# Two transformer layers with mixture-of-experts on one core: the shared expert moved into the last stage, and gathers held to two in flight

## The chip, the cores and the metric

The kernel runs on 1 core of one Trainium2 chip. The metric is the device time of one execution in microseconds (us). Before the change it is 1326.83 us, the median of 3 runs (1325.98 to 1328.25).

The core has five engines with instruction queues of their own: TensorE (PE in the profile, with its weight loads as PEld), VectorE (DVE), ScalarE (ACT), GpSimd (POOL) and SyncE (SP, used only to issue DMAs). They wait for each other through semaphores: a finished instruction adds 1, a landed DMA adds 16. A queue is in order, so whatever stands behind a waiting instruction waits too.

## The reference, cut to what matters

The input is x with 4 x 512 tokens of 256 values. The program computes, in order:

```python
x0 = layernorm(x)           # layer 0: attention with 16 heads, and a mixture of 32 experts, 4 per token
x  = x + attn0(x0) + moe0(x0)
x1 = layernorm(x)           # layer 1: attention (4 heads) and a mixture of experts on the same normalised input
xf = rmsnorm(x1) * norm_w
routed = sum over the token's 4 experts of weight * (silu(xf @ w1[e]) * (xf @ w3[e])) @ w2[e]
shared = (silu(xf @ shared_gate_w) * (xf @ shared_up_w)) @ shared_down_w
out = x + x1 + attn1(x1) + routed + shared
```

Each expert has 256 slots in layer 1; a token that finds its expert full is dropped there. The change is about `shared` and about how `routed` is collected at the end. `routed` needs, for each token, the four rows that its experts wrote, times the token's four weights.

## The kernel before, in words

A program is a row of blocks, and all engines meet in a barrier between two of them. In order: `norm_block0`, `route_block` (layer 0), `attention_block0` for batches 0 and 1, `expert_block` (layer 0), `attention_block0` for batches 2 and 3, `norm_block1`, `route_block` (layer 1), `attention_block1`, `expert_block` (layer 1), `combine_block1`. The order inside a block is written out by hand for each engine, and it is the order of the loops in the code. There is no planner.

Tokens lie in 16 tiles of 128; a batch has four of them. `s.x` is the residual in SBUF, `s.xn` the normalised input of the experts, with tokens on the partitions. `xfT` is the same with columns on the partitions, as TensorE wants it; it is made by 32 transpositions of 128 x 128.

**norm_block1** (its body is printed below). SP issues 15 loads: the raw query weights, a bias, norm weight and gate (`w_in`), the three weights of the shared expert (`w_in` too, lines 1349 to 1351), and then the attention's other weights (`attn_in`). VectorE normalises (L1393) and makes `s.xn` (L1401). TensorE transposes both (L1441), ScalarE copies them out (L1416), TensorE computes the logits (L1426). POOL waits for all ten `attn_in` loads, adds up the query weights of four groups (L1368 to L1370, and three small ones for the bias) and then adds the normalised input to the residual (L1377, four instructions).

**route_block, layer 1**. VectorE finds each token's four experts, counts and ranks with TensorE's help, and has the slots ready at L744. Only then can POOL scatter the rows of `s.xn` into `xs` in HBM: 64 indirect DMAs (L761), of which 24 stand in this block and 40 in `attention_block1`. In the same block TensorE projects queries, keys and values of each batch (`project`, L599 and L604), VectorE takes them out (`take`), ScalarE makes their high parts (L513, L515), POOL their low parts (L471, L472), and SP stores all six parts of a batch in HBM. POOL's order is: low parts of batch 0; then for each further batch eight scatters and the two low parts.

The shared expert stands in this block as well, batch by batch: `gate_up` on TensorE (L613), Silu on ScalarE (L523), the product `hidden` on VectorE (L664), `down` on TensorE (L623) and the add to the residual `add_down` on VectorE (L670).

**attention_block1** and **expert_block** compute attention and the routed experts; the latter writes one row per slot into `ys` in HBM.

**combine_block1** is the last stage. POOL issues 64 indirect DMAs (L1700), tile by tile and choice by choice, each of which gathers 128 rows of 256 values from `ys` into a place of its own in `big_a`. VectorE waits for the four gathers of a tile and adds them to the residual with their weights (L1712). SP stores the output two tiles at a time (L1693). TensorE and ScalarE have nothing to do there.

Of the kernel before, what the change touches and what calls it, by code (L numbers as in the profile page):

```python
# [20 lines left out]
ALU = mybir.AluOpType  # L21
# [300 lines left out]

def shared_weights(s):

    w = s.probs[:].rearrange("p a n -> p (a n)")
    at = 0
    views = []
    for width in (EMB, KC * EXPERTS, KC * I1, KC * I1, EMB):
        views.append(w[:, at:at + width])
        at += width  # L330
    nw, gate, sg, su, sd = views
    gate, sg, su = (a.rearrange("p (k n) -> p k n", k=KC) for a in (gate, sg, su))
    return nw, gate, sg, su, sd
# [10 lines left out]
def route_block(nc, s, d, layer, xs_zeroed=None):  # L344
# [51 lines left out]
    else:  # L396
        _, _, sg, su, sd = shared_weights(s)
        xfT = s.big_b[:, 0:KC * TOKENS].rearrange("p (k n) -> p k n", k=KC)
        silu, hid = s.probsT[:, 0:2 * SEQ].rearrange("p (a n) -> p a n", a=2), s.khb
# [3 lines left out]
        UP_BANK, V_BANK, Q_BANK, KA_BANK, KB_BANK, GATE_BANK = s.ps[2:8]  # L403
        DOWN_BANKS = (RANK, small)
        q_full, k_full = s.big_a[:, 0:SEQ], s.big_a[:, SEQ:2 * SEQ]

    with signals(nc, f"r{layer}") as sem, ExitStack() as ctx:
# [7 lines left out]
        projected, taken, gated, silu_done, hid_ready, down_done, x_added = map(  # L415
            sem, ("projected", "taken", "gated", "silu", "hid", "down", "x_added"))
# [67 lines left out]
        def _(act):  # L484
# [22 lines left out]
            else:  # L507
# [10 lines left out]
                split_high(0)  # L518
                for c in range(BATCH):
                    act.wait_ge(gated, c + 1)  # L520
                    if c >= 2:
                        act.wait_ge(hid_ready, c - 1)
                    a(silu[:, c % 2], GATE_BANK[:, :], ACT.Silu).then_inc(silu_done, 1)  # L523
                    if c + 1 < BATCH:
                        split_high(c + 1)

        @block.tensor
        def _(pe):
# [79 lines left out]
            def gate_up(c):  # L608
                if c:
                    pe.wait_ge(hid_ready, c)  # L610
                for bank, wt in ((GATE_BANK, sg), (UP_BANK, su)):
                    for k in range(KC):
                        mm = nc.tensor.matmul(bank[:, :], wt[:, k, :], xfT[:, k, c * SEQ:(c + 1) * SEQ],  # L613
                                              start=k == 0, stop=k == KC - 1)
                mm.then_inc(gated, 1)

            def down(c):
                pe.wait_ge(hid_ready, c + 1)
                for half, bank in enumerate(DOWN_BANKS):
                    if c:  # L620
                        pe.wait_ge(x_added, 2 * (c - 1) + half + 1)
                    for i in range(2):
                        mm = nc.tensor.matmul(bank[:, i * EMB:(i + 1) * EMB],  # L623
                                              hid[:, c % 2, (2 * half + i) * P:(2 * half + i + 1) * P], sd,
                                              start=True, stop=True)
                    mm.then_inc(down_done, 1)

# [3 lines left out]
            gate_up(0)  # L631
            tile_row()
            for b in range(1, BATCH):
                project(b)
                if b == 1:
                    pe.wait_ge(row_read, 1)
                down(b - 1)
                gate_up(b)
            down(BATCH - 1)

        @block.vector
        def _(dve):
# [16 lines left out]

            def hidden(c):  # L660
                dve.wait_ge(silu_done, c + 1)
                if c >= 2:
                    dve.wait_ge(down_done, 2 * (c - 1))
                v.tensor_tensor(hid[:, c % 2], silu[:, c % 2], UP_BANK[:, :], ALU.mult).then_inc(hid_ready, 1)  # L664

            def add_down(c):
                for half, bank in enumerate(DOWN_BANKS):
                    dve.wait_ge(down_done, 2 * c + half + 1)
                    t = 4 * c + 2 * half
                    v.tensor_tensor(s.x[:, t:t + 2, :], s.x[:, t:t + 2, :],  # L670
                                    bank[:, :].rearrange("p (t e) -> p t e", t=2), ALU.add).then_inc(x_added, 1)
# [645 lines left out]
def norm_block1(nc, s, d):  # L1317
# [4 lines left out]
    nw, gate, sg, su, sd = shared_weights(s)  # L1322
# [4 lines left out]
    with signals(nc, "n1") as sem, ExitStack() as ctx:  # L1327
# [9 lines left out]
        def _(sp):  # L1337
# [21 lines left out]
            sp.wait_ge(w_in, 16 * 5)  # L1359
# [20 lines left out]
        def _(dve):  # L1380
# [17 lines left out]
            dve.wait_ge(w_in, 16 * 5)  # L1398
# [20 lines left out]
        def _(pe):  # L1419
            def logits(c):  # L1420

                pe.wait_ge(w_in, 16 * 5)
# [257 lines left out]

def combine_block1(nc, s, d):
    gath = s.big_a[:, 0:TILES * TOPK * EMB].rearrange("p (j e) -> p j e", j=TILES * TOPK)
    with signals(nc, "m") as sem, ExitStack() as ctx:  # L1683
        x_added, y_stored = sem("x_added"), sem("y_stored")
        gathered = [sem(f"gathered{t}") for t in range(TILES)]
        block = ctx.enter_context(nc.Block())
# [154 lines left out]
```

## Time and profile before

| what | before |
|---|---|
| median of 3 runs | 1326.83 us (1325.98 to 1328.25) |
| the profiled execution | 1326.87 us, its span 1325.7 us |
| mean granted TensorE clock | 0.921 of full speed |
| busy over the span: PE, PEld | 83%, 62% |
| busy over the span: DVE, ACT, POOL | 59%, 39%, 39% |

The profile page divides the span into 40 slices of 33 us and gives the busy share of each engine in tenths:

```profile
PE   5669999999949999588889999959679979999100
DVE  4868776665115555599997766257337545545233
ACT  2336665555204444355555565131123324444000
POOL 0657776555000000555665564043634300000575
PEclk9879999999969999799999999979969979999655
```

How to read it: a 9 is 90% or more, and a 0 next to none. The last three slices are the last stage: TensorE 0, POOL 5 to 7. The second route stage is around slice 28. PEclk is the clock that the chip granted to TensorE, in tenths of its full speed (2.4 GHz); 5 is the lower level, 1.2 GHz.

### The profile page before, as it was taken

Reading aid. Unit: us, or ns where it says so; the run is one execution under the profiler, and the core shown is the slowest. Engines: PE = TensorE matmul, PEld = TensorE weight load, DVE = VectorE, ACT = ScalarE, POOL = GpSimd, SP = SyncE. Lnnn points to the kernel's source line nnn. Section 1 sums busy time; section 2 is a strip of 40 time slices with the busy share of each in tenths; the row PEclk is TensorE's granted clock in tenths of the full one; section 3 lists DMA queues with packets and bytes.
Section 4 is the critical chain, followed back from the end, with each engine's and each line's share of the span. In section 5 each row is a group of like instructions: output and inputs, shape, how many; then the busy total and the mean of one; then the engine's idle time right before and its main releaser. Section 6 shows DMA issues by size and latency. Waiting matters only on the chain. (4 is left out here: it accounts for less than half of the span.)

```text
span 1325.7 us, 19842 instructions
## 1 busy us (share of the span) xinstructions
PE 1098.2 (83%) x5536; PEld 826.1 (62%) x5538; DVE 782.9 (59%) x1925; ACT 521.8 (39%) x1419; POOL 510.9 (39%) x487
## 2 busy tenths in 40 slices
PE   5669999999949999588889999959679979999100
PEld 5436667777838988355557777855357658888100
DVE  4868776665115555599997766257337545545233
ACT  2336665555204444355555565131123324444000
POOL 0657776555000000555665564043634300000575
PEclk9879999999969999799999999979969979999655
DMA  9432232221456555322222221025578235554343
GB/s 358 186 100 84 92 92 77 76 76 49 191 129 181 179 180 164 108 72 76 78 75 68 79 72 34 1 83 230 182 225 279 95 92 164 161 164 155 102 133 106
DMA packets 116214, 167.21 MB, mean 126 GB/s; under 512 B 15136, under 2 KB 88736, under 8 KB 113952
## 3 DMA queue, kind: packets, MB, share of 16 engines
q1 hardware_dynamic: 76464, 107.46, 25.9%
q0 software_dynamic: 12288, 33.57, 7.9%
q10 hardware_dynamic: 27360, 24.92, 5.4%
q8 instruction: 52, 0.85, 0.3%
q14 instruction: 50, 0.41, 0.1%
HBM read 103.11 MB, written 62.78 MB: 125 GB/s over the span
## 5 line engine op out<-in xcount | busy, mean ns | idle before, releaser
L1211 PE MATMUL bank<-big_a,probsT 128*128 x760 | 199.4, 358 | 0.4 <-DVE probsT L1283 0.4
L856 POOL TENSOR_TENSOR parts<-wq,parts 128x256 fp32r<-128x256 f32 x64 | 49.0, 766 | 382.1 <-ACT parts L1101 382.1
L1110 ACT ACTIVATE probs<-bank,negmax 128x256 f32<-128x256 f32 (+3 forms) x256 | 134.7, 536 | 123.1 <-DVE negmax L1025 114.6
L917 PE MATMUL bank<-kT,qT 128*128 128x256 f32 (+3 forms) x512 | 171.7, 457 | 0.0
L933 PE MATMUL bank<-const,probs 128*128 128x128 f32 x640 | 129.7, 276 | 27.7 <-DVE probs L1037 27.6
L949 PE MATMUL bank<-probsT,big_b 128*128 128x512 f32 (+3 forms) x512 | 149.0, 434 | 0.0
L1289 DVE TENSOR_TENSOR work<-work,bank 128x96 f32<-128x96 f32 (+1 forms) x190 | 51.5, 271 | 159.3 <-ACT work L1256 159.3
L1211 PEld LDWEIGHTS bank<-big_a,probsT 128*128 128x128 f32 x760 | 130.7, 193 | 21.1 <-issue 2.1
L1025 DVE TENSOR_REDUCE negmax<-bank 128x1 f32<-128x256 f32 (+3 forms) x256 | 113.6, 486 | 47.1 <-PE bank L919 46.0
L1700 POOL DMA_INDIRECT big_a<-ys_dram,slot_r x64 | 61.6, 963 | 200.5 <-PEq L1683 181.3
L901 PE MATMUL bank<-parts 128*128 128x512 f32 x256 | 116.9, 492 | 19.8 <-POOL parts L856 15.2
L1123 ACT ACTIVATE probsT<-bank,kh 128x512 f32<-128x512 f32 (+3 forms) x256 | 118.1, 527 | 21.0 <-PE bank L933 15.9
L1201 PE MATMUL bank<-const,probs 128*128 128x128 f32 x380 | 104.5, 278 | 21.4 <-DMA probs<-xs_dram 21.4
L949 PEld LDWEIGHTS bank<-probsT,big_b 128*128 128x128 f32 x512 | 85.9, 190 | 51.2 <-issue 23.5
L1037 DVE TENSOR_SCALAR probs<-probs,rsum 128x512 f32<-128x512 f32 (+3 forms) x256 | 116.0, 515 | 2.3
L955 PE MATMUL bank<-big_b,big_a 128*128 128x256 f32 x512 | 116.3, 379 | 0.0
L917 PEld LDWEIGHTS bank<-kT,qT 128*128 128x128 f32 x512 | 83.3, 193 | 47.3 <-issue 36.4
L933 PEld LDWEIGHTS bank<-const,probs 128*128 128x128 f32 x640 | 84.0, 142 | 45.7 <-DVE probs L1037 32.4
L955 PEld LDWEIGHTS bank<-big_b,big_a 128*128 128x128 f32 x512 | 96.7, 190 | 12.7
L1263 ACT ACTIVATE work<-bank 128x256 f32<-128x256 f32 x190 | 72.8, 383 | 71.0 <-PE bank L1229 70.8
L1256 ACT ACTIVATE work<-bank 128x96 f32<-128x96 f32 (+1 forms) x190 | 50.1, 264 | 125.7 <-PE bank L1211 125.7
L761 POOL DMA_INDIRECT xs_dram<-xn,slot_w x64 | 63.2, 987 | 75.3 <-DVE shift L1622 45.0
(208 smaller groups left out, 2022.8 us busy)
## 6 DMA issues: line engine op xcount, KB each, us to landing
probs<-xs_dram SPq DMA_DIRECT2D x190, 128.0 KB
ys_dram<-work ACTq DMA_DIRECT2D x190, 128.0 KB
work<-khT_dram SPq DMA_DIRECT2D x64, 256.0 KB
xs_dram<-big_a SPq DMA_DIRECT2D x12, 1024.0 KB, 19.5
wq<-in_wq SPq DMA_DIRECT2D x64, 128.0 KB
big_a<-in_gu SPq DMA_DIRECT2D x1, 6144.0 KB, 18.3
stack_dram<-parts SPq DMA_DIRECT2D x24, 256.0 KB
xlow<-stack_dram SPq DMA_DIRECT2D x48, 128.0 KB
```

The lines of the kernel that those rows point to most:

```text
L901: mm = nc.tensor.matmul(s.ps[6][:, :], w_parts[wp][:, u % 2, k, :], (x_high, x_low)[xp][bi][:, k, :], start=n == 0, stop=last)
L917: nc.tensor.matmul(s.ps[bank][:, at:at + w], s.qT[:, par, i * P:(i + 1) * P], s.kT[:, par, 0:w], start=True, stop=False)
L933: mm = nc.tensor.transpose(s.ps[bank][:, at + (i - j) * P:at + (i - j + 1) * P], s.probs[:, par, ROW_AT[i] + j * P:ROW_AT[i] + (j + 1) * P ...
L949: mm = nc.tensor.matmul(s.ps[7][:, j * P:], s.vp[:, rows[u // H0] * ROWS + j, :], s.probsT[:, COL_AT[j]:COL_AT[j] + w], start=n == 0, stop ...
L955: mm = nc.tensor.matmul(s.ps[bank][:, 0:EMB], s.oT[bi][:, h, i * P:(i + 1) * P], s.wout[:, h, :], start=h == 0, stop=h == H0 - 1)
L1025: v.tensor_reduce(s.negmax[:, par, i:i + 1], s.ps[bank][:, at:at + (i + 1) * P], AX.X, ALU.max, negate=True).then_inc(maxed, 1)
L1037: v.tensor_scalar(row, row, s.rsum[:, par, i:i + 1], None, ALU.mult).then_inc(prob_ready, 1)
L1110: nc.scalar.activation(s.probs[:, par, ROW_AT[i]:ROW_AT[i] + (i + 1) * P], s.ps[bank][:, at:at + (i + 1) * P], ACT.Exp, bias=s.negmax[:, p ...
L1123: nc.scalar.activation(s.probsT[:, COL_AT[j]:COL_AT[j] + w], s.ps[bank][:, at:at + w], ACT.Copy, scale=s.kh[:, rows[bi] * ROWS + j, H0 + h ...
L1201: mm = nc.tensor.transpose(s.ps[i % 2][:, k * P:(k + 1) * P], rows_in[:, i % UNROLL, k * P:(k + 1) * P], s.c("ident"))
L1211: mm = nc.tensor.matmul(s.ps[2 + i % 2][:, 0:W], rowsT[:, i % 2, k * P:(k + 1) * P], gu[:, k, bass.ds(e * W, W)], start=k == 0, stop=k == ...
L1263: nc.scalar.activation(outs[:, j], s.ps[6 + i % 2][:, 0:EMB], ACT.Copy).then_inc(out_ready, 1)
```

## The change

The shared expert leaves `route_block` and comes into `combine_block1`; its weights are loaded there, into a free part of `big_a`, and not in `norm_block1` any more. `xfT` is overwritten in between (its place holds expert weights), so the last stage makes it again from `s.xn`: 32 transpositions on TensorE, eight copies on ScalarE. VectorE does the product of batch 0 before it combines the first tile, and the later ones after every fourth tile; it adds the shared expert's result to a pair of tiles after it has combined them. In the route block, project(1) takes the place that gate_up(0) had in TensorE's order. The gathers now have one semaphore for each choice k and not for each tile, and each gather waits until the one two places before it has landed. VectorE waits for each gather by itself.

```diff
@@ route_block, layer 1
                 weights()
-                split_high(0)
-                for c in range(BATCH):
-                    act.wait_ge(gated, c + 1)
-                    if c >= 2:
-                        act.wait_ge(hid_ready, c - 1)
-                    a(silu[:, c % 2], GATE_BANK[:, :], ACT.Silu).then_inc(silu_done, 1)
-                    if c + 1 < BATCH:
-                        split_high(c + 1)
+                for b in range(BATCH):
+                    split_high(b)
...
             project(0)
             count_and_rank()
             ends()
-            gate_up(0)
+            project(1)
             tile_row()
-            for b in range(1, BATCH):
+            for b in range(2, BATCH):
                 project(b)
-                if b == 1:
-                    pe.wait_ge(row_read, 1)
-                down(b - 1)
-                gate_up(b)
-            down(BATCH - 1)
...
             for b in range(1, BATCH):
-                hidden(b - 1)
                 take(b)
-                add_down(b - 1)
-            hidden(BATCH - 1)
-            add_down(BATCH - 1)
@@ norm_block1
-            sp.dma_start(sg, kchunks(d["sg1"])).then_inc(w_in, 16)
-            sp.dma_start(su, kchunks(d["su1"])).then_inc(w_in, 16)
-            sp.dma_start(sd, d["sd1"]).then_inc(w_in, 16)
...
-            sp.wait_ge(w_in, 16 * 5)
+            sp.wait_ge(w_in, 16 * 2)
@@ combine_block1
         @block.sync
         def _(sp):
+            sp.dma_start(sg, d["sg1"].rearrange("(k p) n -> p k n", p=P)).then_inc(w_in, 16)
+            sp.dma_start(su, d["su1"].rearrange("(k p) n -> p k n", p=P)).then_inc(w_in, 16)
+            sp.dma_start(sd, d["sd1"]).then_inc(w_in, 16)
             out = d["out"].rearrange("(t p) e -> p t e", p=P)
             for g in range(TILES // 2):
-                sp.wait_ge(x_added, 2 * TOPK * (g + 1))
+                sp.wait_ge(combined, 2 * TOPK * (g + 1))
+                sp.wait_ge(shared_added, g + 1)
                 sp.dma_start(out[:, 2 * g:2 * g + 2], s.x[:, 2 * g:2 * g + 2]).then_inc(y_stored, 16)
...
             for t in range(TILES):
                 for k in range(TOPK):
+                    before = t + (k >= 2)
+                    if before:
+                        pool.wait_ge(gathered[(k + 2) % TOPK], 16 * before)
                     nc.gpsimd.indirect_dma_start(
                         out=gath[:, t * TOPK + k], out_offset=None, in_=d["ys"],
                         in_offset=bass.IndirectOffsetOnAxis(ap=s.slot_r[:, k, t:t + 1], axis=0),
-                    ).then_inc(gathered[t], 16)
+                    ).then_inc(gathered[k], 16)
+
+        @block.tensor
+        def _(pe):
...
+            for g in range(TILES // 4 * KC):
+                turn(g)
+            pe.wait_ge(w_in, 16 * 3)
+            for c in range(BATCH):
+                gate_up(c)
+                down(c)
...
+        @block.scalar
+        def _(act):
+            a = nc.scalar.activation
+            for g in range(TILES // 4 * KC):
+                act.wait_ge(turned, g + 1)
+                a(xfT[:, g % KC, g // KC * 512:(g // KC + 1) * 512], s.ps[g % 4][:, :], ACT.Copy).then_inc(xfT_ready, 1)
+            for c in range(BATCH):
...
+                a(silu[:, c % 2], GATE_BANK[:, :], ACT.Silu).then_inc(silu_done, 1)
...
+            def combine(t):
+                for k in range(TOPK):
+                    dve.wait_ge(gathered[k], 16 * (t + 1))
+                    if k:
+                        dve.wait_ge(combined, TOPK * t + k)
+                    v.scalar_tensor_tensor(out=s.x[:, t, :], in0=gath[:, t * TOPK + k], scalar=s.weight[:, t, k:k + 1],
+                                           in1=s.x[:, t, :], op0=ALU.mult, op1=ALU.add).then_inc(combined, 1)
...
+            def add_down(c, half):
+                dve.wait_ge(down_done, 2 * c + half + 1)
+                t = 4 * c + 2 * half
+                dve.wait_ge(combined, TOPK * (t + 2))
+                v.tensor_tensor(s.x[:, t:t + 2, :], s.x[:, t:t + 2, :],
+                                DOWN_BANKS[half][:, :].rearrange("p (t e) -> p t e", t=2), ALU.add).then_inc(shared_added, 1)
+
+            hidden(0)
             for t in range(TILES):
+                c, i = divmod(t, ROWS)
+                combine(t)
+                if i % 2:
+                    add_down(c, i // 2)
+                if i == 3 and c + 1 < BATCH:
+                    hidden(c + 1)
```

`turn`, `gate_up`, `down` and `hidden` of the last stage have the bodies that stand in the norm and route blocks; `gate_up` also waits for ScalarE's copies.

## Rows read from the trace of the kernel before

**Rows 1.** The chain of waits over the last 90 us, by line.
```profile
by line: POOL big_a L1700 66.2%; issue 21.9%; DMA big_a<-ys_dram,slot_r 3.0%; DVE x_res L1712 2.2%; POOLq L1683 1.4%
```
**Rows 2.** Stretches: length, busy of PE, PEld, DVE, ACT, POOL, clock, DMA, GB/s.
```profile
916.80:955.40 38.60, 32.38 (x122) 19.38 (x120) 16.82 (x27) 5.57 (x9) 31.69 (x30) 1.00 0.53 191
1236.10:1317.00 80.90, 0.00 (x0) 0.00 (x0) 29.16 (x60) 0.00 (x0) 61.62 (x64) 0.50 0.43 125
```
**Rows 3.** Groups by line: busy us, mean ns; idle before, by releaser.
```profile
L1700 POOL DMA_INDIRECT big_a<-ys_dram,slot_r x64 | 61.6, 963 | 200.5 <-PEq L1683 181.3 <-issue 19.2
```
**Rows 4.** Last stage in order of time: start us, duration us, instruction.
```profile
1236.17 0.98 POOL L1700 DMA_INDIRECT big_a<-ys_dram,slot_r  x1 [181.29 <-PEq L1683]
1237.45 0.96 POOL L1700 DMA_INDIRECT big_a<-ys_dram,slot_r  x1 [0.30 <-issue]
...
1249.83 71.39 SPq L1693 DMA_DIRECT2D out<-x_res  x8
1249.97 0.95 POOL L1700 DMA_INDIRECT big_a<-ys_dram,slot_r  x1 [0.30 <-issue]
...
1253.33 2.10 DVE L1712 SCALAR_TENSOR_TENSOR x_res<-big_a,weight,x_res 128x256 f32<-128x256 f32 x4 [3.53 <-DMA big_a<-ys_dram,slot_r]
...
1315.92 1.06 POOL L1700 DMA_INDIRECT big_a<-ys_dram,slot_r  x1 [0.30 <-issue]
1318.77 2.05 DVE L1712 SCALAR_TENSOR_TENSOR x_res<-big_a,weight,x_res 128x256 f32<-128x256 f32 x4 [2.60 <-DMA big_a<-ys_dram,slot_r]
```
**Rows 5.** Line 1700, first gather alone (1236 to 1237): start to landing.
```profile
DMA to landing us min/median/max: 2.8/2.8/2.8
```
**Rows 6.** The chain of waits in order of time, at the last gather.
```profile
1315.92 2.74 DMA big_a<-ys_dram,slot_r
```
**Rows 7.** Route stage in order of time, VectorE and POOL.
```profile
915.86 0.20 DVE L744 TENSOR_SCALAR slot_r<-slot_w 128x64 int32<-128x64 int32 x1
916.89 1.02 POOL L761 DMA_INDIRECT xs_dram<-xn,slot_w  x1 [8.03 <-DVE slot_r L744]
...
954.07 1.27 POOL L472 TENSOR_TENSOR parts<-big_a,parts 128x512 fp32r<-128x512 f32 x1
```
**Rows 8.** Groups by line and form, 830 to 960 us.
```profile
L761 POOL DMA_INDIRECT xs_dram<-xn,slot_w x24 | 24.2, 1007 | 14.8 <-DVE slot_r L744 8.0 <-issue 6.7
L613 PE MATMUL bank<-big_b,probs 128*128 128x512 f32 x32 | 14.5, 595 | 0.0
L623 PE MATMUL bank<-probs,work 128*128 128x256 f32 x32 | 7.7, 383 | 1.4 <-issue 1.4
L670 DVE TENSOR_TENSOR x_res<-x_res,bank 128x512 f32<-128x512 f32 x8 | 5.2, 682 | 1.4 <-PE bank L623 1.2 <-issue 0.2
L664 DVE TENSOR_TENSOR work<-probsT,bank 128x512 f32<-128x512 f32 x4 | 2.7, 682 | 3.7 <-ACT probsT L523 2.4 <-issue 1.3
```
**Rows 9.** Norm stage in order of time, SP's queue, VectorE and POOL.
```profile
873.17 0.43 SPq L1343 DMA_DIRECT2D big_a<-in_bkb  x1
...
873.04 6.42 DVE L1401 SCALAR_TENSOR_TENSOR xn<-big_a,kh,probs 128x256 f32<-128x256 f32 x16
...
876.97 3.08 POOL L1368 TENSOR_TENSOR big_a<-big_a 128x256 f32<-128x256 f32 x1 [59.21 <-DMA big_a<-in_bkb]
880.13 0.64 POOL L1369 TENSOR_TENSOR big_a<-big_a 128x256 f32<-128x256 f32 x1
...
882.37 9.60 POOL L1377 TENSOR_TENSOR x_res<-x_res,big_a 128x1024 f32<-128x1024 f32 x4
```
**Rows 10.** Layer 1 attention in order of time, a scatter that waits for VectorE.
```profile
995.24 0.69 DVE L1622 TENSOR_TENSOR shift<-const,negmax 128x512 fp32r<-128x512 f32 x1
...
996.71 0.97 POOL L761 DMA_INDIRECT xs_dram<-xn,slot_w  x1 [2.52 <-DVE shift L1622]
```
**Rows 11.** Line 1683, the last block's end: duration ns min/median/max, start.
```profile
L1683 POOLq DRAIN  x1: 20570/20570/20570, 1301.7 to 1301.7; - x1
L1683 SPq COMPARE_BRANCH  x1: 33/33/33, 1323.0 to 1323.0; - x1
```

More of the change, by code:

```diff
@@ L606, in project @@
                 mm.then_inc(projected, 1)
[L608 to L626, printed above, removed]
             project(0)
@@ L1321, in norm_block1 @@
     xfT = s.big_b[:, 0:KC * TOKENS].rearrange("p (k n) -> p k n", k=KC)
[L1322 removed]
+    nw, gate = route_weights(s)
     rms = s.kh[:, 0, 0:TILES]
@@ L1682, in combine_block1 @@
     gath = s.big_a[:, 0:TILES * TOPK * EMB].rearrange("p (j e) -> p j e", j=TILES * TOPK)
+    sg, su, sd = shared_weights(s)
+    xfT = s.big_b[:, 0:KC * TOKENS].rearrange("p (k n) -> p k n", k=KC)
+    silu, hid = s.probsT[:, 0:2 * SEQ].rearrange("p (a n) -> p a n", a=2), s.khb
+    GATE_BANK, UP_BANK, DOWN_BANKS = s.ps[4], s.ps[5], (s.ps[6], s.ps[7])
     with signals(nc, "m") as sem, ExitStack() as ctx:
-        x_added, y_stored = sem("x_added"), sem("y_stored")
-        gathered = [sem(f"gathered{t}") for t in range(TILES)]
+        w_in, combined, shared_added, y_stored = map(sem, ("w_in", "combined", "shared_added", "y_stored"))
+        turned, xfT_ready, gated, silu_done, hid_ready, down_done = map(
+            sem, ("turned", "xfT", "gated", "silu", "hid", "down"))
+        gathered = [sem(f"gathered{i}") for i in range(TOPK)]
         block = ctx.enter_context(nc.Block())
@@ L1702, in _, with turn, gate_up, down @@
                         in_offset=bass.IndirectOffsetOnAxis(ap=s.slot_r[:, k, t:t + 1], axis=0),
-                    ).then_inc(gathered[t], 16)
+                    ).then_inc(gathered[k], 16)
+        @block.tensor
+        def _(pe):
+            def turn(g):
+                c, k = g // KC, g % KC
+                if g >= 4:
+                    pe.wait_ge(xfT_ready, g - 3)
+                for i in range(4):
+                    mm = nc.tensor.transpose(s.ps[g % 4][:, i * P:(i + 1) * P], s.xn[:, 4 * c + i, k * P:(k + 1) * P],
+                                             s.c("ident"))
+                mm.then_inc(turned, 1)
+            def gate_up(c):
+                pe.wait_ge(xfT_ready, KC * (c + 1))
+                if c:
+                    pe.wait_ge(hid_ready, c)
+                for bank, wt in ((GATE_BANK, sg), (UP_BANK, su)):
+                    for k in range(KC):
+                        mm = nc.tensor.matmul(bank[:, :], wt[:, k, :], xfT[:, k, c * SEQ:(c + 1) * SEQ],
+                                              start=k == 0, stop=k == KC - 1)
+                mm.then_inc(gated, 1)
+            def down(c):
+                pe.wait_ge(hid_ready, c + 1)
+                for half, bank in enumerate(DOWN_BANKS):
+                    if c:
+                        pe.wait_ge(shared_added, 2 * (c - 1) + half + 1)
+                    for i in range(2):
+                        mm = nc.tensor.matmul(bank[:, i * EMB:(i + 1) * EMB],
+                                              hid[:, c % 2, (2 * half + i) * P:(2 * half + i + 1) * P], sd,
+                                              start=True, stop=True)
+                    mm.then_inc(down_done, 1)
+            for g in range(TILES // 4 * KC):
[4 more added lines that the diff above has]
+                down(c)
@@ L1705, in _ @@
         @block.vector
         def _(dve):
-            for t in range(TILES):
-                dve.wait_ge(gathered[t], 16 * TOPK)
-                for k in range(TOPK):
-                    if k:
-                        dve.wait_ge(x_added, TOPK * t + k)
-                    nc.vector.scalar_tensor_tensor(out=s.x[:, t, :], in0=gath[:, t * TOPK + k],
-                                                   scalar=s.weight[:, t, k:k + 1], in1=s.x[:, t, :],
-                                                   op0=ALU.mult, op1=ALU.add).then_inc(x_added, 1)
+            v = nc.vector
```

49 lines of the change are left out of this document (22 added, 27 removed).

## The prediction

> **What bounds the kernel now.** Only three stages are touched, so I read each by itself. The share of busy time on the page would not do: it mixes stages in which TensorE works without a pause with a last stage in which it does nothing. I looked first at the chain of waits over the last 90 us: two thirds of it are POOL's gather instructions and a fifth is the pause in front of each [rows 1]. The table by stretches says the same: in the 80.9 us from 1236.1 to 1317.0 POOL is busy for 61.6 us and VectorE for 29.2 us, while TensorE and ScalarE have no instruction at all [rows 2]. The list of groups gives the pace: 64 gathers of 0.963 us with 19.2 us of pauses in 63 gaps, 0.305 us each, so one gather about every 1.25 us [rows 3]. The order of time confirms it: first gather 1236.17, last 1315.92, that is 79.75 us for 63 steps [rows 4]. Nothing holds a gather back today except the instruction before it. The reader should see there that this stage is an issue loop on POOL, and that a store of the output or a slow combine costs nothing until the tail.
>
> The second thing to read is how long one gather takes to land: the first one, with nothing before it in the queue, 2.8 us from its start [rows 5]; the last one 2.74 us [rows 6]. Both are longer than two steps of 1.25 us. At today's pace there are always a little more than two under way. That is what decides this change.
>
> The second route stage is also POOL's. It starts its scatters at 916.89, when the slots are ready (L744 ends at 916.06), and ends its last subtraction at 954.07 + 1.27 = 955.34 [rows 7]. In 38.6 us POOL is busy 31.7 us [rows 2], and what is missing is the pause before each of the 24 scatters: 6.7 us [rows 8]. TensorE is busy too, 32.4 us, with a part that is the shared expert's, but nobody on POOL's chain waits for it there.
>
> **What leaves the route stage.** TensorE loses 14.5 us of gate and up matmuls (L613) and 7.7 us of down matmuls (L623); VectorE loses 2.7 us of products (L664) and 5.2 us of adds (L670) [rows 8]; ScalarE loses four Silu. I price all of it at 0. The cover is POOL's run of 24 scatters and six subtractions, which needs 38.5 us from the slots to the end whatever the others do. Before the slots VectorE sets the time, without the shared expert in its way: the first product L664 starts only after L744. Project(1) now stands ahead of the transposition of the expert row on TensorE, and takes about as long as the other projections; its result is wanted by VectorE right after the slots, and POOL asks for batch 1 only after eight scatters, some 10 us later. If the cover were gone, the last batch's quarter of TensorE's 22.2 us would be saved at the end, 5.6 us; a loss I don't see, since only work leaves. I take 0, with bounds 0 and -1 for POOL meeting VectorE less often; the 5.6 us is a rival below.
>
> **What leaves the norm stage.** Three weight loads of 128 KB go from the middle of SP's list. Each issue costs 0.4 to 0.5 us of SP's queue, so the last small load, now issued at 873.17, goes out about 1.5 us earlier, and POOL, which waits for all attention weights and starts at 876.97, could start at about 875.5. The stage does end with POOL: its four additions to the residual run from 882.37 to 891.97 [rows 9]. So it looks like a gain of 1.5 us. I do not count it: POOL's first addition (L1368) took 3.08 us where the next one of the same form took 0.64. It ended at 880.05, which is 0.6 us after the end of VectorE's run of L1401 at 873.04 + 6.42 = 879.46 [rows 9]. L1401 reads two tensors from SBUF, and POOL got its turn when that run was over. An earlier start would only lengthen the wait. The run itself starts when ScalarE's and VectorE's own chain lets it, not when the weights land, so it stays where it is. By the first reading the term is -1.5 us, by the second 0; I take 0 and keep both.
>
> The Trainium skill (SBUF — State Buffer, "Who interferes with whom") says the same in general: a VectorE instruction with two SBUF inputs contends with a GpSimd instruction that reads SBUF. It speaks against the gain that the loads alone promise.
>
> **What the last stage gets beside the gathers.** Here TensorE transposes 32 blocks, runs gate, up and down, and ScalarE copies eight banks and does four Silu; VectorE gets four products and eight adds. At the lower clock, 0.50 in that stretch [rows 2], I double the 22.2 us of TensorE to 44, and about 10 us for the transpositions make 55 us at most, in a stage of over 80. VectorE's 29.2 us become 37. The first product stands ahead of the first combine in VectorE's order and may hold it back by some 10 us at the start; VectorE then has 16 tiles to catch up, and no gather waits for it, since each gather has its own place in the buffer. Cost of all that: 0. Without cover it would be that late start, once. Three weight loads of 128 KB share the DMA engines with the first gathers: 0.3 us.
>
> **Two gathers in flight.** Each gather from the third on now waits until the one two places before has landed. On POOL every later gather is queued behind the waiting one, and VectorE's combine and at last the store wait for those. So two steps cost: start to landing, and landing to the start of the next gather on POOL. The first is 2.74 to 2.8 us [rows 5, 6]. The second is not in the trace for a gather. The nearest row is a scatter that waited for VectorE: L1622 ends at 995.24 + 0.69 = 995.93 and the scatter starts at 996.71, 0.78 us later [rows 10]. Compare the 0.30 us when nothing is waited for [rows 3]: a waiting indirect DMA is set off only after its signal. Bounds: 0.30 below, 0.90 above (0.78 and the 0.11 us that VectorE took from landing to start, 1318.66 to 1318.77 [rows 4, 6]). I take 0.78, the only row of this kind. A pair then takes 2.74 + 0.78 = 3.52 us. Gather 64 is 31 pairs and one step of 1.28 us behind the first: 31 x 3.52 + 1.28 = 110.4 us instead of 79.75. That is **+30.7 us**. With the lower bound 31 x 3.04 + 1.28 = 95.5, +15.8; with the upper bound and 2.8 to land, 31 x 3.70 + 1.28 = 116.0, +36.2.
>
> **Stores in the way.** Gathers under way beside a store of the output land later: the one at 1249.97, issued 0.14 us after a store, let VectorE start at 1253.33, 3.36 us later, against 2.85 us for the last [rows 4]. That 0.5 us cost nothing before; now it holds up one of the two interleaved sequences. Seven stores of 0.5 us, half of which reaches the end: **+1.7 us**; bounds 0 and 7.
>
> **Tail.** Before, four combines of 0.49 us (29.16 / 60 [rows 2]) stood behind the last landing, from 1318.77 to about 1320.8. Now only one does (0.48 us), and one add of 0.68 us (L670's form [rows 8]) before the last store: 0.83 us less. POOL's own drain, which ended 6.35 us after the start of the last gather (1301.7 + 20.57 = 1322.27), is then as late as the store (1323.0 before [rows 11]), so **-0.7 us**.
>
> **Sum.** 30.7 + 1.7 - 0.7 + 0 + 0 = +31.7, less than 0.3 for the loads in either direction. The profiled execution took 1326.87 us (span 1325.7), the median of the three runs is 1326.83, so no correction: 1358.5, I say 1358.
>
> **A page against the rows.** The Trainium skill (DMA: Bandwidth & Descriptors, "Anatomy of one DMA — SWDGE (gpsimd) path") gives about 2.0 us plus bytes over 436 GB/s for a DMA issued from GpSimd, 2.3 us for 128 KB; with it a pair would take 3.08 us, the stage +17 us, and the kernel about 1345. The row on a gather with nothing before it says 2.8, so the sum goes by the row.
>
> **Rivals.**
> 2. *Long landings.* A gather that starts alone, and the stores, make 3.25 us the usual landing (3.36 less 0.11). A pair takes 4.03 us, +46: about 1372. For it: the 3.36 us that the trace has. Against it: that gather stood beside a store, and there is one store for eight gathers. Chance 0.07.
> 3. *The wait is already met: the other side.* If the landing itself is long today only because the DMA queue is filled at 1.25 us a gather, two in flight would land earlier. From a landing of 1.72 us (two steps of 1.25 less 0.78) no gather waits any more, the stage keeps its 79.75 us, the tail gives 0.7 and the norm stage perhaps 1.5: 1324.6, faster. Against it: the very first gather had an empty queue and took 2.8. Chance 0.04.
> 4. *The route stage gives some back.* If the matmuls of the shared expert, and not POOL, set the end of each batch, the last batch's 5.6 us leave it, and the kernel lands near 1353. Against it: POOL has no gap between L744's end and 955.34 but its own pauses. Chance 0.03.
>
> **How the numbers follow.** My forecast has 0.66, with its own range 1352 to 1366 (restart 0.6 to 0.9, stores 0 to 6). 0.03 is left for what I don't see. The range for 8 in 10 reaches down to the quick restart and leaves out most of the long landings: 1343 to 1366. About 0.2% (2.7 us) is what a measurement of this kernel can tell from no change. Faster by more than that 0.03, within it 0.03, slower 0.94.
>
> **What would show it.** In the changed kernel's groups the gather's pauses must rise from 19 us in total to about 50, with the landing DMA as releaser, and the first and last gather must lie about 112 us apart; gather starts must come in two interleaved sequences with about 3.5 us between every second one. POOL's L1368 must end near 880 although it starts earlier, and the route stage must still end with POOL's subtraction 38 to 39 us after the slots. A landing that shrinks below 2.5 us, or a gather that starts 0.3 us after the landing it waited for, would prove me wrong; so would a combine that waits for VectorE's own product late in the stage.

## The result, and the profile after

The changed kernel takes 1346.31 us (median of 4 runs, 1345.18 to 1347.59); the kernel before, on the same chip, 1326.67 us (4 runs, 1325.98 to 1328.25). The ratio is 1.0147, with an interval of 1.0129 to 1.0164: slower by 19.6 us. The direction was forecast and the time lies in the range, but 1358 was 12 us too much. The first rival (quick restart, 1343 to 1344) came closer than the forecast.

The profiled execution took 1346.62 us (span 1344.7) against 1326.87, so there are 19.75 us to account for. The page after, engines in 40 slices and the chain that ended last:

```profile
PE   5669999999949999688889999777199799998421
DVE  4867876566115554799997776364256444553433
ACT  2336675555114444355555554120033234444000
POOL 0657776554000000665655562046444200001665
PEclk9879999999969999799999999988589899999765
...
DMA big_a<-ys_dram,slot_r 7%; POOL big_a L1663 0%; DVE x_res L1741 0%; DVE x_res L1728 0%; POOLq L1637 0%; DVEq L1740 0%; POOLq L156 0%
```

In the last three slices TensorE now has some work, and the chain has changed hands: before, two thirds of the last 90 us were POOL's gather instructions [rows 1], now it is the landing of gathers. The list of groups for the last stage shows the same (busy us, mean ns | idle before, by releaser):

```profile
L1663 POOL DMA_INDIRECT big_a<-ys_dram,slot_r x64 | 66.7, 1041 | 215.2 <-POOLq L156 181.2 <-DMA big_a<-ys_dram,slot_r 31.9 <-issue 2.1
L1728 DVE SCALAR_TENSOR_TENSOR x_res<-big_a,weight,x_res 128x256 f32<-128x256 f32 x64 | 30.9, 484 | 55.6 <-DMA big_a<-ys_dram,slot_r 54.9
L1685 PE MATMUL bank<-big_b,big_a 128*128 128x512 f32 x32 | 15.4, 626 | 0.0
```

Against [rows 3]: the 19.2 us of plain pauses became 2.1, and 31.9 us of waiting for a landing stand in their place, 14.8 us more in all; the mean gather grew from 963 to 1041 ns, 5.1 us for the 64. The two stretches (POOL is the fifth busy time, the last three numbers are granted clock, DMA share and GB/s), to be held against [rows 2]:

```profile
918.40:957.20 38.80, 18.45 (x56) 9.79 (x56) 9.05 (x15) 3.78 (x6) 31.96 (x30) 0.69 0.52 190
1237.80:1338.60 100.80, 32.64 (x95) 20.13 (x93) 37.00 (x73) 6.74 (x12) 66.65 (x64) 0.65 0.36 104
```

TensorE was busy for 18.45 us instead of 32.38 in the route stage, which still lasts as long as before. Its granted clock fell there too, from 1.00 to 0.69 of full speed. That cost nothing: the route stage is POOL's, and from its end to the first gather it is 280.7 us against 280.8. In the last stage the granted clock is 0.65 instead of 0.50. Gathers and combines in order of time (start us, us, engine, line):

```profile
1237.87 0.98 POOL L1663 DMA_INDIRECT big_a<-ys_dram,slot_r  x1 [181.16 <-POOLq L156]
...
1241.07 0.94 POOL L1663 DMA_INDIRECT big_a<-ys_dram,slot_r  x1 [0.96 <-DMA big_a<-ys_dram,slot_r]
...
1326.35 0.48 DVE L1728 SCALAR_TENSOR_TENSOR x_res<-big_a,weight,x_res 128x256 f32<-128x256 f32 x1 [1.27 <-DMA big_a<-ys_dram,slot_r]
1326.58 1.07 POOL L1663 DMA_INDIRECT big_a<-ys_dram,slot_r  x1 [0.69 <-DMA big_a<-ys_dram,slot_r]
...
1337.47 1.07 POOL L1663 DMA_INDIRECT big_a<-ys_dram,slot_r  x1 [0.34 <-DMA big_a<-ys_dram,slot_r]
```

First to last gather: 1337.47 - 1237.87 = 99.60 us, against 79.75 [rows 4]. The chain in order of time (start us, us, what) gives the step itself:

```profile
1323.11 0.26 issue
1323.37 2.95 DMA big_a<-ys_dram,slot_r
1326.32 0.26 issue
1326.58 2.86 DMA big_a<-ys_dram,slot_r
```

**The 19.75 us.** Gathers, first to last: +19.85. The first gather starts 1237.87 - 1236.17 = 1.70 later; 1.29 of that was there before the norm stage, whose first VectorE instruction starts at 866.59 instead of 865.30, in code that the change does not touch, 0.27 is the route stage (38.72 instead of 38.45 us), and 0.14 is spread over the rest. From the last gather to SP's last branch: 1343.8 - 1337.47 = 6.33 against 7.08, -0.75. After that branch: 1346.62 - 1343.8 = 2.82 against 3.87, -1.05, for which no row gives a reason. Sum +19.75.

### The profile page after: what moved, and what is told of

It is laid out like the page before. It is cut to its first block and busy times, and to the rows that moved or that the text cites. A ratio compares the mean times of both kernels' runs of the same rounds, so it can differ in the third digit from the quotient of the medians.

```text
span 1344.7 us, 19981 instructions
## 1 busy us (share of the span) xinstructions
PE 1117.1 (83%) x5570; PEld 837.2 (62%) x5570; DVE 781.9 (58%) x1925; ACT 523.8 (39%) x1425; POOL 516.2 (38%) x487
## 5 line engine op out<-in xcount | busy, mean ns | idle before, releaser
L1663 POOL DMA_INDIRECT big_a<-ys_dram,slot_r x64 | 66.7, 1041 | 215.2 <-POOLq L156 181.2
L854 PE MATMUL bank<-parts 128*128 128x512 f32 x256 | 117.5, 494 | 19.6 <-POOL parts L809 15.1
L990 DVE TENSOR_SCALAR probs<-probs,rsum 128x512 f32<-128x512 f32 (+3 forms) x256 | 115.4, 514 | 2.3
```

The costliest lines, as they stand in the source:

```text
L854: mm = nc.tensor.matmul(s.ps[6][:, :], w_parts[wp][:, u % 2, k, :], (x_high, x_low)[xp][bi][:, k, :], start=n == 0, stop=last)
L990: v.tensor_scalar(row, row, s.rsum[:, par, i:i + 1], None, ALU.mult).then_inc(prob_ready, 1)
```

## The experiments

Times are medians, and each is held against the kernel before, timed beside it on the same chip.

**1 and 2: the wait without the move, and the move without the wait.** The first keeps the shared expert in the route stage and adds to the kernel before the limit, its semaphores, and VectorE's wait for each gather by itself:

```diff
-        gathered = [sem(f"gathered{t}") for t in range(TILES)]
+        gathered = [sem(f"gathered{i}") for i in range(TOPK)]
...
+                    before = t + (k >= 2)
+                    if before:
+                        pool.wait_ge(gathered[(k + 2) % TOPK], 16 * before)
...
-                    ).then_inc(gathered[t], 16)
+                    ).then_inc(gathered[k], 16)
...
-                dve.wait_ge(gathered[t], 16 * TOPK)
                 for k in range(TOPK):
+                    dve.wait_ge(gathered[k], 16 * (t + 1))
```

The second undoes just that in the changed kernel.

> The kernel before with one part of the change alone: gathers two in flight, one semaphore per choice, VectorE waiting gather by gather; the shared expert stays in the route stage. Theory A (the wait is the whole price, a pair of gathers takes the landing of 2.8 us and a restart of about 0.35 us): the gathers spread over 98 to 101 us instead of 79.75, the kernel at 1345 to 1347. Rival B (the shared expert beside the gathers takes part of the 19.6 us): with the shared expert away the kernel is at 1335 to 1342. My forecast's own step (restart 0.78 us) would give 1356 to 1358 and is already in doubt.

> The changed kernel without the limit on gathers: one semaphore per tile as before, no wait on POOL; the shared expert stays in the last stage. Theory A: gathers 1.25 us apart again, the kernel within 2 us of before (1325 to 1329). Rival B: 5 to 12 us slower than before.

Measured: the limit alone 1347.13 us (1346.04 to 1348.77) against 1326.27, ratio 1.0155 (1.0139 to 1.017). The move alone 1327.75 us (1326.05 to 1331.06), ratio 1.0014 (1.0004 to 1.0025); its gathers span 80.2 us and have their plain pauses again:

```profile
L1660 POOL DMA_INDIRECT big_a<-ys_dram,slot_r x64 | 61.9, 967 | 200.5 <-POOLq L156 181.3 <-issue 19.2
```

So the limit is the whole price, and the move costs about 0.14%, near what can be told from nothing. VectorE's wait gather by gather came together with the limit in the first kernel; experiment 3 has that wait too and costs nothing, so it is not what costs. With the limit alone the gathers span 102.4 us, more than the 99.6 of the full change. The landings in its chain show why (start us, us):

```profile
1251.33 3.44 DMA big_a<-ys_dram,slot_r
...
1277.42 3.38 DMA big_a<-ys_dram,slot_r
...
1290.51 3.46 DMA big_a<-ys_dram,slot_r
...
1329.87 3.49 DMA big_a<-ys_dram,slot_r
```

Every 13 us, which is a store's eight gathers, one landing takes 0.5 us longer. In the changed kernel's chain one landing alone is of that kind (3.63 us at 1303.80).

**3 and 4: three in flight, and one.**

```diff
-                    before = t + (k >= 2)
-                    if before:
-                        pool.wait_ge(gathered[(k + 2) % TOPK], 16 * before)
+                    n = t * TOPK + k - 3
+                    if n >= 0:
+                        pool.wait_ge(gathered[n % TOPK], 16 * (n // TOPK + 1))
```

(- 1 in place of - 3 for one in flight.)

> The changed kernel with three gathers in flight instead of two. Theory A: three steps of 1.25 us are 3.75 us, more than landing and restart (3.15), so hardly any gather waits: the kernel within 2 us of before, 1325 to 1328, a bit better than without a limit since VectorE combines gather by gather and only one combine stands behind the last landing. Rival B: 5 to 12 us slower. If a limit cost something by itself (each wait instruction on POOL), 64 waits of 0.1 us would show as 6 us.

> The changed kernel with one gather in flight. Measures landing and restart by themselves, with nothing else of POOL's under way. Theory A: 63 steps of 3.15 us, 198 us between first and last gather, the kernel at about 1445. If the landing of a gather with an empty queue is shorter than 2.8 us (2.3), a step takes 2.65 and the kernel is at 1413. If the restart is 0.78 us, 3.6 us a step, 1473.

Three in flight: 1327.67 us (1325.31 to 1330.81), ratio 1.0009 (1.0000 to 1.0018), gathers over 81.9 us. The group shows that the wait is nearly always met; in the chain it holds a gather up three times, behind landings of 3.54 to 4.95 us:

```profile
L1663 POOL DMA_INDIRECT big_a<-ys_dram,slot_r x64 | 61.6, 963 | 202.5 <-POOLq L156 181.3 <-issue 17.7 <-DMA big_a<-ys_dram,slot_r 3.5
```

One in flight: 1444.64 us (a single execution), gathers over 198.9 us. It is the cleanest measure of a step, since nothing overlaps:

```profile
1239.58 0.96 POOL L1663 DMA_INDIRECT big_a<-ys_dram,slot_r  x1 [2.52 <-DMA big_a<-ys_dram,slot_r]
1242.63 0.94 POOL L1663 DMA_INDIRECT big_a<-ys_dram,slot_r  x1 [2.10 <-DMA big_a<-ys_dram,slot_r]
...
1302.30 0.48 DVE L1728 SCALAR_TENSOR_TENSOR x_res<-big_a,weight,x_res 128x256 f32<-128x256 f32 x1 [2.64 <-DMA big_a<-ys_dram,slot_r]
1302.53 1.07 POOL L1663 DMA_INDIRECT big_a<-ys_dram,slot_r  x1 [2.05 <-DMA big_a<-ys_dram,slot_r]
...
1305.63 1.07 POOL L1663 DMA_INDIRECT big_a<-ys_dram,slot_r  x1 [2.02 <-DMA big_a<-ys_dram,slot_r]
```

Alone, a step is 3.05 us: 2.79 to land and, by its chain, 0.26 to restart. Once a combine starts with the gather (VectorE 0.23 us before POOL), the gather instruction takes 1.07 us instead of 0.94 and the step 3.10 in the rows shown, 3.16 in the mean of all such steps, those beside stores included. So about 0.1 us of each step goes with the combine beside it. That the two coincide is shown; that SBUF is what they share is not.

**5: why the scatter's row misled.** The restart in the sum came from a scatter [rows 10], which checks its indices against a bound. Here the gathers get a bound too, with the same data moved:

```diff
+                        bounds_check=USED_TILES * P - 1, oob_is_err=False,
```

> The changed kernel, each gather with a bounds check on its row numbers as the scatter has, so that the registers for the bound are set between the wait and the gather. Theory A (the scatter's restart of 0.78 us is long because of what stands between wait and DMA): restart near 0.8 us, a pair of gathers 3.55 to 3.65 us, the kernel at 1358 to 1362. Rival: the restart depends on who gives the signal (a landing against VectorE), then it stays near 0.35 us and the kernel at 1346 to 1348.

Measured: 1361.94 us (1361.41 to 1363.26) against 1328.24, ratio 1.0258 (1.0237 to 1.0279); gathers over 115.4 us, (115.4 - 1.28) / 31 = 3.68 a pair. The queue of POOL now holds a register instruction per gather, and the chain shows what it does to a restart:

```profile
L1663 POOLq MOVE  x64: 29/29/29, 1236.3 to 1351.8; - x64
```

```profile
1271.45 2.83 DMA big_a<-ys_dram,slot_r
1274.28 0.02 issue
1274.31 0.03 POOLq L1663
1274.34 0.70 issue
1275.04 2.77 DMA big_a<-ys_dram,slot_r
```

From landing to start it is 0.76 us, near the scatter's 0.78, where the unbounded gather needs 0.26: 0.50 us more at 31 joints, or 15.5 of the 15.8 us by which the gathers take longer. The bound by itself adds little: a gather whose wait was already met follows its predecessor after 0.30 us as before, and the instruction takes 1.00 us. The longer restart shows only after a wait, and the MOVE is what now stands between wait and DMA. The bound and its MOVE came together, though, so that it is the MOVE is argued from its place; what the 0.70 us consists of, the trace does not show.

This run shows one thing more. Its combines start at the landing and are over when the gather starts 0.76 us after it, and the landings that no store disturbs take 2.81 us in the mean of its chain, against 2.88 in the changed kernel's.

**6: the norm stage.** The prediction gave nothing for POOL's earlier loads. In this kernel POOL waits for the two loads of its first four additions only, so that they cannot be late:

```diff
-            load("raw_q", kchunks(d["wq1"]), KC)
-            load("bq", d["bq"])
+            sp.dma_start(raw_q_in, kchunks(d["wq1"])).then_inc(q_in, 16)
+            sp.dma_start(bq, d["bq"]).then_inc(q_in, 16)
...
-            pool.wait_ge(attn_in, 16 * 10)
+            pool.wait_ge(q_in, 16 * 2)
```

> The changed kernel, where POOL in the norm stage waits only for the two loads that its additions read (raw query weights and bias), not for all ten. Theory A (VectorE's run of L1401 with two SBUF inputs kept POOL out, and an earlier start than that run helps): POOL's small additions are over before 874, the stage ends 3 to 6 us earlier, though POOL's long additions then hold VectorE back in turn: the kernel at 1340 to 1344. Rival (the first addition is slow whenever it comes, about 3 us, and POOL's chain is just moved): the stage ends 6 to 8 us earlier with L1401 undisturbed, 1338 to 1340. If nothing is gained because the long additions wait for VectorE's run anyway: 1346.

Measured: 1351.17 us (1347.73 to 1351.31) against 1328.24, ratio 1.0168 (1.0149 to 1.0187), where the changed kernel has 1.0147; that is 3 to 5 us more, and every theory missed. The rows of the changed kernel, and then of this one:

```profile
874.33 6.42 DVE L1351 SCALAR_TENSOR_TENSOR xn<-big_a,kh,probs 128x256 f32<-128x256 f32 x16
877.84 3.50 POOL L1318 TENSOR_TENSOR big_a<-big_a 128x256 f32<-128x256 f32 x1 [58.80 <-DMA big_a<-in_bkb]
...
883.66 9.60 POOL L1327 TENSOR_TENSOR x_res<-x_res,big_a 128x1024 f32<-128x1024 f32 x4
```

```profile
870.42 12.62 DVE L1345 TENSOR_SCALAR big_a<-x_res,meanvar,rstd 128x256 f32<-128x256 f32 x16
871.64 0.74 POOL L1320 TENSOR_TENSOR big_a<-big_a 128x256 f32<-128x256 f32 x1 [51.05 <-DMA big_a<-in_bq]
...
874.74 4.82 POOL L1329 TENSOR_TENSOR x_res<-x_res,big_a 128x1024 f32<-128x1024 f32 x2
...
883.23 8.52 DVE L1353 SCALAR_TENSOR_TENSOR xn<-big_a,kh,probs 128x256 f32<-128x256 f32 x16
```

POOL's first addition needs 0.74 us when VectorE's two-tensor run is not on: the 3.08 of [rows 9] was waiting. But now POOL's large additions fall on VectorE's earlier run, which takes 12.62 us instead of 5.25. The median instruction of that run still takes 0.41 us, the longest 2.49, about as long as one large addition of POOL (2.4 us): a few instructions carry the whole delay. The first scatter comes at 924.72 instead of 918.44, and 1.54 us of that was there when the norm stage began. POOL's order was harmless as it stood because it stood in VectorE's shadow.

**7 to 12: can the uncovered route stage be used?** The move takes TensorE's load out of the route stage, POOL's scatters cover that. With half of the scatters there and half beside attention it should shrink:

```diff
-EARLY_TILES = 6
+EARLY_TILES = 3
...
-                    for t in (2 * b - 2, 2 * b - 1):
+                    for t in range((b - 1) * EARLY_TILES // 3, b * EARLY_TILES // 3):
```

It was run in the kernel before (twice), and in the changed kernel with three in flight (twice), without limit, and with two.

> The kernel before with only three of the sixteen tiles scattered in the route stage (12 scatters instead of 24), the others in the attention stage. Takes POOL's cover off the shared expert. Theory A (POOL sets the route stage, and with half its scatters away the chain of TensorE, VectorE, ScalarE does): the route stage 8 to 11 us shorter, the attention stage 0 to 4 us longer, the kernel at 1317 to 1323. Rival (the attention stage pays it back in full): 1326 to 1330.

> The changed kernel with three gathers in flight and only three tiles scattered in the route stage. Against the run before it, it prices the shared expert in the route stage once POOL doesn't cover it. Theory A: without the shared expert each batch's chain is 3 to 5 us shorter there, the kernel at 1308 to 1317, 5 to 10 us below the kernel before with the same scatters. Rival (the moved work never was on the route stage's path): equal to the run before it within 2 us.

> The changed kernel without a limit on gathers and with three tiles scattered in the route stage. In the run with three in flight and the same scatters the front part was about 7 us shorter (route stage -15, attention +8), but in the last stage signals from TensorE to ScalarE and VectorE came 8 to 36 us late and the end was lost. Theory A (that lateness comes with the waits on POOL, or with gather-by-gather combining): here it is gone and the kernel at 1318 to 1322. Rival (it comes with the shared expert's matmuls beside gathers at 1.25 us, whenever the stages before are laid out this way): again 1335 to 1345.

> The changed kernel as it is (two gathers in flight), with three tiles scattered in the route stage. Theory A: front part 7 us shorter, last stage as in the change: 1337 to 1341. If the late signals come here as well, they stay hidden as long as they are shorter than the 15 to 20 us by which the gathers are slower: the same time, with idle time of ScalarE in the last stage put down to no known releaser. If they are longer, 1345 or more.

> The kernel before with three tiles scattered in the route stage, once more: the first time its runs fell into two groups (1304.6 once, 1322 to 1330 else), with an attention stage 8 us longer in the profiled one. The same scatters in the changed kernel without a limit gave 1312.0 with an attention stage of unchanged length. Theory A (the shared expert in the route stage costs 8 us there once POOL doesn't cover it, 31.6 against 23.5 us): 1318 to 1321, 7 to 8 us above the run without a limit. Rival (the slow attention stage belongs to this layout): again 1325 to 1329.

> The changed kernel with three gathers in flight and three tiles scattered in the route stage, once more, beside the run above. If the late signals of the first time were an incident: 1310 to 1313. If they belong to this kernel: 1336 to 1345 again, with ScalarE's wait for an unknown releaser in the last stage.

| kernel | median us | before us | route stage us | to the last scatter us | gathers us |
|---|---|---|---|---|---|
| before, 3 tiles early (7) | 1326.92 (1304.58 to 1329.8) | 1328.24 | 31.7 | 107.1 | 80.2 |
| the same again (11) | 1325.42 (1319.89 to 1328.57) | 1327.73 | 31.7 | 106.7 | 80.0 |
| changed, three in flight (8) | 1338.2 (1336.3 to 1344.85) | 1328.24 | 23.5 | 106.4 | 79.4 |
| the same again (12) | 1336.0 (1334.13 to 1338.66) | 1327.73 | 23.5 | 104.9 | 80.1 |
| changed, no limit (9) | 1312.0 (1310.44 to 1315.12) | 1326.48 | 23.5 | 97.6 | 80.4 |
| changed, two in flight (10) | 1329.86 (1327.93 to 1333.62) | 1326.48 | 23.5 | 97.3 | 100.0 |

("To the last scatter" is the time from the end of the route stage to the start of POOL's last scatter in the attention stage; the kernel before has 98.6 there, the changed one too. For 7, 11 and 12 medians are compared: their ratios lean on single executions of 1304.58 and 1304.75 us, for which I have no explanation.)

Experiment 9 beats both kernels: ratio 0.9894 (0.9876 to 0.9912), 14.5 us faster than before. With two in flight it is 1.0029 (1.0017 to 1.004): the early tiles give the change some 16 us back, and the limit takes 17.9. Both came out better than expected, since the attention stage was not longer as it had been in 8. With 12 scatters the route stage is 31.7 us with the shared expert in it and 23.5 without, so 8.2 us is what the move is worth in that stage where nothing covers it. The kernel before does not profit: its route stage shrinks by 6.8 us, the median by 1 to 2 us; the rest is lost again in attention, which is some 8 us longer. The scatters that moved there are not the reason, since 9 and 10 have the same ones and an attention stage of unchanged length.

Experiments 8 and 12 are held up in the last stage in a way no theory has. Two of the last stage's four Silu in 8:

```profile
1264.92 0.60 ACT L1717 ACTIVATE probsT<-bank 128x512 f32<-128x512 f32 x1 [26.71 <-remote]
1309.86 0.60 ACT L1717 ACTIVATE probsT<-bank 128x512 f32<-128x512 f32 x1 [44.34 <-remote]
```

and the waits of ScalarE for the Silu in 12, then in 9 (us in total, times, longest):

```profile
ACT probsT L1717 <- remote: 80.2, 3, 43.5
```

```profile
ACT probsT L1714 <- PE bank L1682: 46.4, 4, 19.8
```

In 8 and 12 two of the Silu start 16 to 36 us after the matmuls that they wait for have ended, and the profile names no releaser ("remote"). In 8 all gathers have landed by about 1312, while the last add of the shared expert ends at 1336.4. It came back in the second run, so it belongs to this kernel; 3, 9 and 10, each of which shares a part of its edit, do not have it in this stage.

Such waits are not confined to the last stage. In the attention stage of 11:

```profile
ACT work L1664 <- remote: 5.7, 2, 5.4
```

The runs 7, 8, 11 and 12 have waits of ScalarE of this kind in attention, and they are the four whose attention stage is 6 to 9 us longer; the kernels before and after, 9 and 10 have none (6 has a single one, of 2.7 us). So the lost gain of the kernel before and the misses of 8 and 12 may have one cause. No run isolates it: **it is open.**

## Why the prediction was right and where it was wrong

**The wait as the whole price: right.** Experiment 1 has it alone. That TensorE, VectorE, loads and combines of the moved expert cost about nothing beside the gathers is experiment 2; TensorE was busy for 32.6 us in the last stage, where the prediction allowed 55.

**Landing plus restart, the step that failed.** The sum took 2.74 + 0.78 a pair, 110.4 us in all; measured is (99.60 - 1.28) / 31 = 3.17, of which the chain gives 0.26 to the restart at each of its joints and 2.91, the mean of the rest, to the landing. The landing was a little under-sized (+0.17 x 31 = +5.3), the restart three times over-sized (-0.52 x 31 = -16.1); 110.4 + 5.3 - 16.1 = 99.6. The choice between 0.30 and 0.78 went to the only row of a waiting indirect DMA, though the text had noticed what set that row apart, the bound's register. Experiment 5 puts the bound back and has the scatter's restart again. The prediction had named a gather that starts 0.3 us after its landing as a sign of being wrong, and that is what every joint shows. So rival 1 is the mechanism that came true, even a little below its lower bound of 0.30; its 1343 to 1344 missed by 2.7 mostly because it kept the landing at 2.74. The range reached down to 1343 only because this rival was counted in; the forecast's own 1352 to 1366 does not hold the measured time.

The Trainium skill (Perfetto Trace Analysis, "DMA Instruction — SWDGE (GPSIMD)") has the instruction decoded and queued before its semaphore wait; the 0.26 us agrees with it. The Trainium skill's price for a landing (DMA: Bandwidth & Descriptors, "Anatomy of one DMA — SWDGE (gpsimd) path"), 2.3 us for 128 KB as an estimate from its fixed and its per-byte part, stays below the 2.79 us of experiment 4 at its least disturbed. With that and the slow restart the prediction noted 1345, close to the measured time through two errors of opposite sign.

**Stores, +1.7: a real mechanism, hardly met here.** Beside a store a landing is 0.5 us longer, seen in the chain at every store beside gathers in experiment 1 but once in the changed kernel, 0.75 us. The place of the store goes with it: in experiment 1 it is issued 0.2 to 0.3 us after the start of the gather that lands late, in experiment 5 0.6 us after. In the changed kernel, where the shared expert's add stands before it, it is issued 0.9 to 1.1 us after one gather's start and 0.3 to 0.9 before the next. That the place decides is my reading, and the one late landing there does not follow from it.

**A term that the sum did not have.** What lengthens the landings in the changed kernel is mostly the combine beside each gather: 1.07 us on POOL instead of 0.94, about 0.1 x 31 = 3 us. With 2.79 instead of 2.74 for an undisturbed landing (1.5 us) and the one late landing, that makes the +5.3. Before, with combines beside the gathers too, the mean was 963 [rows 3]; now both engines wait for the same landing and start within 0.23 us of each other, and the mean is 1041 (1027 in experiment 1). That the common start does it is my reading of the rows in experiment 4. Experiment 5 supports it, where the combine is over before the gather starts and an undisturbed landing takes 0.07 us less, but it changes the bound as well; no run took the combine alone away.

**Tail, -0.7: right**, -0.75 measured. POOL's drain ends at 1337.2 + 6.59 = 1343.79, 6.32 us after the last gather's start (6.35 in the prediction), and is level with SP's branch, as forecast; before, it ended at 1322.27 against 1323.0 [rows 11]:

```profile
L1637 POOLq DRAIN  x1: 6592/6592/6592, 1337.2 to 1337.2; - x1
L1637 SPq COMPARE_BRANCH  x1: 33/33/33, 1343.8 to 1343.8; - x1
```

**Route stage, 0: right.** 38.7 us after 38.45, still POOL's.

**Norm stage, 0: right, and for its reason.** POOL starts 0.42 us earlier in its stage, not the 1.5 of the first reading; its addition takes 3.50 instead of 3.08 us and ends 1.29 later, just as the stage is late. Experiment 6 shows what the shadow hid. The Trainium skill (SBUF — State Buffer, "Who interferes with whom"), which the prediction weighed, agrees with the addition of 0.74 us away from VectorE's two-tensor run and 3.50 beside it. The opposite direction, VectorE's TENSOR_SCALAR run held up by POOL, cost more than the one that I looked at.

**The other rivals.** Long landings: with two in flight only beside stores. Wait already met: it fails with two in flight, but with three it is what happens, since 2.79 + 0.26 = 3.05 lies above two steps of 1.25 and below three. Route stage gives back: not with 24 scatters over it, 8.2 us with 12.

## What to carry to other kernels

Work out a limit on transfers in flight as (landing + restart) over the issue step: here 3.05 / 1.25 = 2.4, so three in flight are all but free (81.9 us against 80.2 without a limit) and two cost a quarter of the stage. Take the restart from a row with the same instructions between wait and DMA. Work moved off an engine that is covered brings nothing until the cover moves too: only the move together with fewer early scatters and no limit was worth 14 us, and with three in flight the same was lost again for a reason that is open.

## What was not expected of the hardware

- With a bound, and so a register MOVE of 29 ns between the wait and an indirect DMA on POOL: 0.76 us from landing to start instead of 0.26.
- VectorE's 16 TENSOR_SCALAR (one tensor from SBUF) took 12.62 us instead of 5.25 beside POOL's additions, with single ones of up to 2.49 us and a median of 0.41, and its two-tensor run 8.52 instead of 6.42.
- A gather instruction takes 1.07 us instead of 0.94 when a combine starts with it.
- In one kernel of this family ScalarE's start came up to 36 us after the matmuls that it waited for, and in four runs of two kernels the same attention code took 6 to 9 us longer. Of the 70 executions of the kernel before that stood beside the experiments one took 1304.75 us, and of the 24 of its variant in 7 and 11 one took 1304.58, some 22 us below the medians beside them. All of this is open.
